# A four-layer gated network on one core: the second layer's gather split into two halves of tokens, and the third layer's attention rebuilt in 512-column units in four PSUM banks

## The reference

```python
# layer 1 (the second), feed-forward: 32 experts, 4 for each token, 256 seats for each expert
out_slots = eo[sorted_eid, pos]                      # every expert's output rows
routed = zeros_like(x).at[tok].add(out_slots * flat_w[order][:, None])
x = x + tanh(g_ffn[1]) * (residual + routed + shared)
# layer 2 (the third), attention: 32 heads of 8 features, against the 128 context rows of the same b
h = layernorm(x)
q = rmsnorm(heads(h @ Wq.T));  k = rmsnorm(heads(ctx @ Wk.T));  v = heads(ctx @ Wv.T)
attn = softmax(q @ k.T * 8**-0.5);  x = x + tanh(g_xattn[2]) * (attn @ v)
# layer 2, feed-forward: 8 experts, each of them on all tokens
```

## Time and profile before

| | us |
|---|---|
| median of 3 runs | 1107.32 (1104.63 to 1112.31) |
| the profiled execution: its own time | 1100.47 |
| its span, from the first to the last instruction | 1098.7 |
| DVE waits for the gather's first tile (L1984), end of the gather's last add | 463.74, 502.56 |
| first scores (L1440) | 535.06 |
| last `x` add of the attention (L2040) ends | 595.57 |
| PE busy of the span, DVE, ACT, POOL | 75%, 61%, 42%, 21% |

### The profile page before, as it was taken

The page is one execution under the profiler, slowest core; times in us unless marked ns, Lnnn a source line. Parts: engine busy times, 40 slices in busy tenths (PEclk is TensorE's granted clock), DMA queues, the critical chain, the costliest instruction groups (busy, mean ns, idle before and its releaser), DMA issues.

```text
span 1098.7 us, 17371 instructions
## 1 busy us (share of the span) xinstructions
PE 829.0 (75%) x6240; PEld 533.4 (49%) x6240; DVE 674.1 (61%) x1366; ACT 458.3 (42%) x850; POOL 233.4 (21%) x247
## 2 busy tenths in 40 slices
PE   4785689995504778403587899973977999999998
PEld 2334445654303666303365456642754566666664
DVE  4968734448752777334555766778876555555554
ACT  2544533442202888302453444423842344444442
POOL 3977224331372000272200000004200000000000
PEclk9776699998656999856597999995976999999999
DMA  9422044421024888430000011110000111111111
GB/s 329 168 72 70 1 133 123 134 83 42 10 101 137 270 281 281 152 99 21 1 17 1 30 58 43 50 35 0 3 16 1 58 44 57 46 54 49 51 43 53
DMA packets 51145, 88.39 MB, mean 80 GB/s; under 512 B 5385, under 2 KB 33417, under 8 KB 51090
## 3 DMA queue, kind: packets, MB, share of 16 engines
q1 hardware_dynamic: 39810, 70.90, 20.9%
q0 software_dynamic: 3072, 8.39, 2.4%
q10 hardware_dynamic: 8208, 8.39, 2.2%
HBM read 64.03 MB, written 23.63 MB: 80 GB/s over the span
## 4 chain that ended last, share of the span: by engine, by line
PE 57%; issue 12%; DVE 11%; POOL 8%; DMA 6%; ACT 4%; SPq 1%; POOLq 0%; ACTq 0%; DVEq 0%
PE ps L1124 27%; PE ps L1140 14%; DMA arena<-seats 3%; POOL arena L653 2%; PE ps L1412 2%; PE ps L1086 2%; PE ps L1426 1%; PE ps L1219 1%; DVE stats L1593 1%; PE ps L1234 1%; POOL k_st L570 1%; POOL k_st L565 1%; DMA ctx_sb<-in_ctx 1%; POOL arena L543 1%; PE ps L1440 1%
## 5 line engine op out<-in xcount | busy, mean ns | idle before, releaser
L1124 PE MATMUL ps<-turned_buf,W 128*128 128x512 f16 x1512 | 353.4, 385 | 8.4 <-DVE W L1751 5.9
L1124 PEld LDWEIGHTS ps<-turned_buf,W 128*128 128x128 f16 x1512 | 149.2, 99 | 168.3 <-issue 12.9
L1140 PE MATMUL ps<-W,arena 128*128 128x256 f16 x1512 | 186.6, 275 | 9.5 <-DVE arena L1746 9.5
L1140 PEld LDWEIGHTS ps<-W,arena 128*128 128x128 f16 x1512 | 148.6, 99 | 53.6 <-issue 8.5
L1739 DVE SCALAR_TENSOR_TENSOR arena<-ps,arena 128x512 f32<-128x512 f32 x126 | 86.7, 689 | 114.0 <-ACT arena L838 113.5
L1746 DVE TENSOR_TENSOR arena<-arena 128x512 f16<-128x512 f32 x126 | 87.6, 695 | 96.9 <-ACT arena L864 92.1
L838 ACT ACTIVATE arena<-ps 128x512 f32<-128x512 f32 x126 | 74.9, 595 | 162.3 <-PE ps L1124 161.9
L864 ACT ACTIVATE arena<-arena 128x512 f16<-128x512 f32 x126 | 79.3, 630 | 134.4 <-DVE arena L1739 70.7
L1086 PE MATMUL ps<-ident,xn 128*128 128x128 f32 x112 | 24.9, 405 | 79.7 <-DVE xn L1617 79.7
L525 POOL TENSOR_TENSOR rstd<-veps,mhalf 128x4 f32<-128x4 f32 x16 | 17.9, 1118 | 280.0 <-DVE veps L1598 280.0
L1206 PE MATMUL ps<-ident,arena 128*128 128x128 f32 x128 | 21.8, 297 | 52.8 <-DMA arena<-seats 52.7
(11 more groups left out here) (328 smaller groups left out, 1276.9 us busy)
## 6 DMA issues: line engine op xcount, KB each, us to landing
W<-in_w SPq DMA_DIRECT2D x79, 384.0 KB, 3.1
seats<-wq ACTq DMA_DIRECT2D x1, 8192.0 KB, 37.1
arena<-seats SPq DMA_DIRECT2D x32, 256.0 KB, 4.3
served<-arena SPq DMA_DIRECT2D x32, 256.0 KB, 2.8
wb<-in_w SPq DMA_DIRECT2D x16, 384.0 KB, 4.3
wb<-routed SPq DMA_DIRECT2D x16, 256.0 KB, 3.9
folded<-W SPq DMA_DIRECT2D x4, 384.0 KB, 2.3
W<-folded SPq DMA_DIRECT2D x4, 384.0 KB, 3.5
```

The lines of the kernel that those rows point to most:

```text
L1124: last = nc.tensor.matmul(bank(2 * g + half), W16[:, k % 2, w, g * D + c * P:g * D + (c + 1) * P], x16[:, i, c, half * HALF:(half + 1) * H ...
L1140: last = nc.tensor.matmul(ps[:, 4 + t // 2, (t % 2) * D:(t % 2 + 1) * D], f_h16[:, k % 2, i, t * S:(t + 1) * S], W16[:, k % 2, w, 2 * D:3 ...
```

## The change

- **Gather.** POOL still issues 32 indirect DMAs in the same order; after tile 4 it makes the power for the first half (`inv_sqrt(4, halves=(0,))`), before tiles 5 to 7. `e_back`, `m_from` and `m_w` move to the end of the arena, away from the attention's tiles, which are now written while the gather runs. DVE: add 0 to 3, statistics of half 0, add 4, normalise half 0, add 5, queries of half 0; adds 6 and 7, statistics and normalisation of half 1, and the queries of half 1 stand inside DVE's attention loop.
- **Queries** are made in two halves (`turn_x`, `queries`, `q2_x`, `q2_square`, `q2_guess`, `q2_squares`, `q2_norm`), in banks 4 to 7. Per b ACT now makes both f16 copies in one instruction of 512 elements (`q2_hi`), and DVE both low parts in one of 512 (`q2_norm`), which waits for ACT; POOL's subtractions and DVE's cast are gone.
- **Attention** runs in banks 0 to 3: a unit is 512 columns (4 heads), 8 units for a b. Its four score matmuls all have the same 32 rows (`i = n % 4`) and fill one bank (n % 2); the product with v has one bank (2); `turn_q2` and `turn_o2` share bank 3. `a2_p` has four buffers.
- **Seats.** `seats` and `served` are read and written as `"(p c) d -> p c d"`: partition p holds seats 2p and 2p+1, so a piece is 2 KB.
- The first weight split of the feed-forward block moves to n = 40 (ACT) and n = 42 (DVE) of 64.

```diff
-                sp.dma_start(e_x[:, k % 3, :, :], seats[...].rearrange("(c p) d -> p c d", p=P))
+                sp.dma_start(e_x[:, k % 3, :, :], seats[...].rearrange("(p c) d -> p c d", c=CT))
-                sp.dma_start(served[...].rearrange("(c p) d -> p c d", p=P), e_y[:, k % 3, :, :])
+                sp.dma_start(served[...].rearrange("(p c) d -> p c d", c=CT), e_y[k % 3])
 POOL
-            inv_sqrt(4)
-            for b in range(B):
-                pool.wait_ge(sem("q2_step"), 3 * b + 2)
-                nc.gpsimd.tensor_tensor(a2_st[:, b, :, 3, :], a2_q[:, b, :, :], a2_st[:, b, :, 0, :], ALU.subtract)
+                if t == 4:
+                    inv_sqrt(4, halves=(0,))
+            inv_sqrt(4, halves=(1,))
 ACT
+            def q2_hi(h):
+                for b in range(4 * h, 4 * h + 4):
+                    act.wait_ge(sem("q2_step"), 2 * b + 1)
+                    nc.scalar.activation(a2_st[:, b, :, 0:2, :], a2_q[:, b, :, :].unsqueeze(2).to_broadcast((P, H2, 2, DH2)),
+                                         ACT.Copy).then_inc(sem("q2_hi"), 1)
+            def p2_exp(n):
+                act.wait_ge(sem("scores"), n + 1)
+                if n >= 4:
+                    act.wait_ge(sem("weighed"), n - 3)
+                nc.scalar.activation(a2_p[:, n % 4, :, :].rearrange("p g s -> p (g s)"), bank(n % 2),
+                                     ACT.Exp, scale=float(DH2) ** -0.5).then_inc(sem("probs"), 1)
+            q2_x(0); q2_square(0); q2_guess(0); q2_hi(0)
+            for n in range(8 * B):
+                if n == 12:
+                    q2_x(1)
+                if n == 16:
+                    q2_square(1)
+                if n == 19:
+                    q2_guess(1)
+                if n == 23:
+                    q2_hi(1)
+                ...
+                p2_exp(n)
 PE
+            def scores_2(n):
+                b, hg, i = n // 8, n % 8 // 4, n % 4
+                if n % 8 == 0:
+                    pe.wait_ge(sem("q2T"), b + 1)
+                if n >= 2:
+                    pe.wait_ge(sem("probs"), n - 1)
+                rows = slice(32 * i, 32 * i + 32)
+                for j in range(4):
+                    last = nc.tensor.matmul(ps[:, n % 2, j * S:(j + 1) * S], k2T[rows, b, 4 * hg + j, :],
+                                            a2_qT[rows, b % 2, 4 * hg + j, :], start=True, stop=True)
+                last.then_inc(sem("scores"), 1)
+            def weigh_v2(n):
+                b, hg, i = n // 8, n % 8 // 4, n % 4
+                pe.wait_ge(sem("probs"), n + 1)
+                if i == 0 and n:
+                    pe.wait_ge(sem("oT"), n // 4)
+                for j in range(4):
+                    last = nc.tensor.matmul(ps[32 * j:32 * j + DH2 + 1, 2, i * S:(i + 1) * S], v2[:, b, 16 * hg + 4 * j + i, :],
+                                            a2_p[:, n % 4, j, :], start=True, stop=True, skip_group_check=True)
+                last.then_inc(sem("weighed"), 1)
+            turn_x(0); queries(0); turn_q2(0)
+            for n in range(8 * B):
+                b = n // 8
+                if n == 10:
+                    turn_x(1)
+                if n == 14:
+                    queries(1)
+                scores_2(n)
+                if n % 8 == 1 and b + 1 < B:
+                    turn_q2(b + 1)
+                if n >= 2:
+                    weigh_v2(n - 2)
+                if n % 8 == 4 and b:
+                    turn_o2(b - 1)
 DVE
+            def q2_norm(h):
+                dve.wait_ge(sem("q2_rms"), h + 1)
+                ...                            # four steps of refinement on 128 norms
+                for b in range(4 * h, 4 * h + 4):
+                    nc.vector.tensor_tensor(a2_q[:, b, :, :], q, a2_n[...], ALU.mult).then_inc(sem("q2_step"), 1)
+                    dve.wait_ge(sem("q2_step"), 2 * b + 1)
+                    dve.wait_ge(sem("q2_hi"), b + 1)
+                    nc.vector.tensor_tensor(a2_st[:, b, :, 2:4, :], a2_q[:, b, :, :].unsqueeze(2).to_broadcast((P, H2, 2, DH2)),
+                                            a2_st[:, b, :, 0:2, :], ALU.subtract).then_inc(sem("q2_step"), 1)
+            for t in range(4):
+                add_back(t)
+            statistics(4, 0); add_back(4); normalise(4, 0); add_back(5)
+            q2_squares(0); q2_norm(0); q2T(0)
+            for n in range(8 * B):
+                if n in (2, 4):
+                    add_back(5 + n // 2)
+                if n == 5:
+                    statistics(4, 1)
+                if n == 8:
+                    normalise(4, 1)
+                if n == 18:
+                    q2_squares(1)
+                if n == 22:
+                    q2_norm(1)
+                if n % 8 == 1 and n // 8 + 1 < B:
+                    q2T(n // 8 + 1)
+                if n >= 5 and n % 4 == 1:
+                    o2T((n - 5) // 4)
+                if n % 8 == 6 and n >= 8:
+                    out_2(n // 8 - 1)
```

More of the change, by code:

```diff
@@ L965, in _ @@
             experts()
[L966 to L980, removed]
+            def q2_x(h):
+                act.wait_ge(sem("turn"), 2 * 4 + h + 1)
+                for c in range(KD):
+                    nc.scalar.activation(xT_of(c, h), bank(4 + c), ACT.Copy).then_inc(sem("turned"), 1)
@@ new lines, in q2_square, with q2_guess @@
+            def q2_square(h):
+                for k in (2 * h, 2 * h + 1):
+                    act.wait_ge(sem("q2_mm"), k + 1)
+                    nc.scalar.activation(a2_q[:, 2 * k:2 * k + 2, :, :].rearrange("p b h d -> p (b h d)"), bank(6 + k % 2),
+                                         ACT.Square).then_inc(sem("q2_sq"), 1)
+            def q2_guess(h):
+                sl = slice(h * P, h * P + P)
+                act.wait_ge(sem("q2_ss"), h + 1)
+                nc.scalar.activation(a2_n[:, 2, sl], a2_n[:, 0, sl], ACT.Ln).then_inc(sem("act_step"), 1)
+                act.wait_ge(sem("act_step"), 2 + h)
+                nc.scalar.activation(a2_n[:, 1, sl], a2_n[:, 2, sl], ACT.Exp, scale=-0.5).then_inc(sem("q2_rms"), 1)
@@ L983, in _ @@
                     down_hi(2, 0)
[L984 to L989, removed]
-                                     ACT.Exp, scale=float(DH2) ** -0.5).then_inc(sem("probs"), 1)
+                p2_exp(n)
             turned_16(5)
@@ new lines, in queries @@
+            def queries(h):
+                pe.wait_ge(sem("turned"), 2 * KD * 4 + KD * (h + 1))
+                if h:
+                    pe.wait_ge(sem("q2_step"), 2 * 4)
+                for t in range(4 * h, 4 * h + 4):
+                    for c in range(KD):
+                        last = nc.tensor.matmul(ps[:, 6 + t % 4 // 2, (t % 2) * D:(t % 2 + 1) * D], xT[:, c, t * S:(t + 1) * S],
+                                                wq2[:, c, :], start=(c == 0), stop=(c == KD - 1))
+                    if t % 2:
+                        last.then_inc(sem("q2_mm"), 1)
@@ L1979, in _, with add_back @@
                 expert_h(k)
-            for t in range(B):
+            def add_back(t):
                 dve.wait_ge(sem("back", t % 2), 16 * TOP1 * (t // 2 + 1))
@@ L1991, in _ @@
             groups = a2_q.rearrange("p b h d -> p (b h) d")
             per = 2 * H2
-            for b in range(4):
-                dve.wait_ge(sem("q2_sq"), b + 1)
-                ins = nc.vector.tensor_reduce(a2_n[:, 0, b * per:(b + 1) * per], groups[:, b * per:(b + 1) * per, :],
-                                              AX.X, ALU.add)
-            link(ins)
-            nc.vector.tensor_scalar(a2_n[:, 0, :], a2_n[:, 0, :], 1.0 / DH2, RMS_EPS, ALU.mult, ALU.add).then_inc(sem("q2_ss"), 1)
```

175 lines of the change are left out of this document (80 added, 95 removed).

## The result

The kernel after takes 1137.54 us in the median of four runs (1135.36 to 1139.47), the kernel before 1109.82 in four (1104.63 to 1115.68). The ratio is 1.0282, 95% interval 1.0245 to 1.0319: slower by 2.8%, above the range that I had given.

What follows compares the result with a forecast made beforehand. Gather (42 us), queries (32.5) and attention (60.5) lie in line. 508.0 + 8 x 9.4 + 4.6 + 9.5 + 5.0 gives 602.3; clock +3.0, pieces -2.4, against 595.57: +7.3, median 1114.6, 8-in-10 range 1098 to 1132.

Steps and rivals of the forecast that it cites:

- Start of half 0: From gather to attention: first half's queries prepared during the gather, first scores at 508.0 against 535.06, 27.0 us won.
- Rival 4: Gather and attention: half 0 ready before 500, so attention units overlap the gather; gain 5 or so more, 1109; chance 0.07.
- Price of a unit: Attention loop, PE: four score matmuls of one row group take 0.33 us, the halved product 0.34; 7.8 us per b.
- Rival 1: Attention units cost by their columns: PE needs 6.0 us per b, 14 us less over the loop, 1100; chance 0.13.
- Rival 3: Attention scores: weight loads in one row group don't overlap, a step 0.10 us, 10 us more, 1125; chance 0.05.
- The new wait: Attention loop: PE's product waits for DVE's copy of the single bank, 0.6 to 0.7 us twice per b, 1.3.
- Half 1 in the loop: Second half's preparation inside the attention loop: 4.6 us of PE work plus 9.5 of stands (range 6 to 15).
- Pieces of 2 KB: Experts' loop: larger pieces of seats and served save 2.4 of 4.4 us of late rows (bounds 0 and 4.4).
- The granted clock: Start of the attention loop: PE at half clock costs 3.0 us (range 0 to 24, all eight b).
- rival 2: Attention loop: clock stays at 0.50 in more than two b, each 3 us more; 1121 to 1136; chance 0.18.

Runs made afterwards that it cites:

- the split preparation's kernel: Kernel before, attention loop untouched, gather, norm and queries made in two halves ahead of it, plus 2 KB pieces: 1097.22 us against 1105.16, ratio 0.9899.

## Why the prediction was wrong

**Start of half 0.** Right to 2.5 us: 510.48 for 508.0, with nothing of the attention beside the gather. The queries at half clock took 2.2 more, and the ACT-DVE turns a little less. Rival 4 didn't happen either: POOL's last gather DMA begins at 500.00, 10 us before the first scores.

**Price of a unit.** Right: 0.32 and 0.34 for my 0.33 and 0.34. Rival 1 didn't happen. Rival 3, that weight loads in one row group don't overlap, would have shown as more than 0.33. So here the sentence of the Trainium skill (TensorE: Matmul & The Clock Gate, Part 3, "What overlaps and what doesn't") doesn't hold as it is worded: four matmuls of one row group start 0.06 us apart, their loads beside them. The paragraph ahead of it in the Trainium skill names, beside other row groups, the background weight buffer as a second way for a load to be pulled ahead, which that sentence leaves out.

**The new wait.** 0.80 in the one case at full clock (I said 0.6 to 0.7, and my terms add up to 0.55), as DVE copied the turned queries first, which I hadn't counted; 0.37 to 0.39 at half, twice a b. It was sized roughly right and is no cause: its removal won 0.9 for a b.

**Half 1 in the loop.** PE stood 2.71 (before 519.62), 5.23 and 0.17 in the three blocks, where I had 3.5, 6.0 and 1.9. The blocks came where I had them and cost 3.3 us less.

**Pieces of 2 KB.** 2.4 forecast, nothing measured.

**The granted clock: the step that failed.** I took 3.0 us, and gave rival 2, in which the clock stays at 0.50 in more than two b, a chance of 0.18. It happened in full: on the profiled executions, for which the sum was made, +37.0 us stands against my +7.3. My reason against it was that PE is still some 80% busy in the second half of the loop; the runs show PE busy for 95 to 100% of 30 us and the clock at half. My reason for it, half clock over the 10 us after each pause, was read from one pause alone; after its pause of 1.72 us (before 572.98) the kernel before has a dip of 3.4 us. My prices were too low as well: I took 3 us for a b, from a factor of 1.3. That factor compared counts of instructions in two stretches with different kinds in them; a b of the units of before takes 10.58 at half clock against 6.39, a factor of 1.7. Here a b of 14.07 against the 9.4 of my sum is 4.7, a factor of 1.5. By that the loop from 544.6 to 630.44, less the stand of 5.23, lost a third of 80.6 us, 27 us (an estimate, as no whole b of the new units was measured at full clock). Put in the place of the 3.0, with the 2.5 of the start, it gives 605.3 + 24 + 2.5 = 632 for the last add, where 630.44 was measured. That is closer than the estimate deserves: it leaves out the half clock before 527.4 and has the blocks 3.3 us too long, and the two errors go against each other. The clock is the only large term. Rival 2's own range, 1121 to 1136, ended just below the result for the same reason, and the range of 8 in 10 cut off its upper part.

**What is shown, and what stays open.** Shown: at the same work, with shorter groups alone, the kernel before stays at half clock and its b takes 11.51 instead of 6.39; three added matmuls for each unit bring the clock back in the kernel after; stands and copy waits don't decide. Open: which property of the short groups it is. Their being short, their changing more often and the array's doing less in the same time were not taken apart. Nor was the opposite run made, long groups in the kernel after with half 1 still in the loop. Open too is why the kernel before itself varies between 1101.55 and 1116.95; the profiled run with the exchanged order of scores ties one such time to a longer dip of the clock.

## What to carry to other kernels

Price a change of matmul shape twice, at either clock, and ask which one the new order will be granted: it can't be read off PE's busy share (full clock here at 89%, half clock at 100%). In a loop of small tiled matmuls at full clock, shortening the groups can cost more than the overlap that it buys: here it took a b from 6.39 to 11.51 us. Splitting the preparation and keeping the long groups gave the gain (some 1% here) without that loss, and pushing the overlap further gave nothing, because the next engines in line were already the bound.

## What the runs showed of the hardware

- A change between scores and products costs 0.10 to 0.11 us at either clock. Full: eight scores take 0.33 with pairs 0.056 apart, and 0.33 - 4 x 0.056 = 0.11. Half: eight take 0.54 (in the split preparation's kernel, 533.55 to 534.08), four in two pairs 0.32 (shorter groups, 577.13 to 577.45), so a pair takes 0.11 and 0.10 is left.
- Four matmuls in one row group (kernel after, from 537.19) start as far apart as four pairs in two (kernel before, from 556.10), 0.056 us. A unit of one row group thus pays full price for half of the scores, at half clock 0.54 against 0.32 for two pairs.
- Two row groups overlap without being issued by turns: eight scores, four of the one group ahead of four of the other, take 0.33 as well.
- PE stays at half clock for 92 to 126 us, busy for up to 100% of a stretch of 30 us; three 128x512 matmuls for each unit brought it to full 6.2 us after the first of them, one for each unit didn't.
- The packets of 2 KB took 84 ns in the median, those of 1 KB 46: 24 against 22 bytes for each ns.
